# Both batches of a head side by side in the query and key rooms, fetched together for the first tile

## The reference, cut to what matters

```python
# L1 attention: 16 heads of 8, two softmaxes for each head
Q, K, V = proj(Wq), proj(Wk), proj(Wv)
Q1, Q2 = split(Q); K1, K2 = split(K)
A1 = where(causal, Q1 @ K1.T * scaling, -inf)
A2 = where(causal, Q2 @ K2.T * scaling, -inf)
attn = softmax(A1) - lam * softmax(A2)
O = attn @ V          # then an rms norm and Wo
```

## Time and profile before

| | us |
|---|---|
| median of 3 runs | 503.64 (502.91 to 507.45) |
| the profiled execution | 507.12 |
| its span, first to last instruction | 505.1 |
| PE busy | 461.2 (91%) |
| DVE busy | 418.5 (83%) |
| ACT busy | 264.7 (52%) |
| POOL busy | 266.7 (53%) |

### The profile page before, as it was taken

How to read it: one execution, slowest core, us unless ns; L and a number is a source line. 1 busy time by engine, 2 the same in 40 slices (tenths; PEclk the granted TensorE clock), 3 DMA queues, 4 the chain that set the end, 5 groups by cost and what they waited for, 6 DMA issues and landing times.

```text
span 505.1 us, 8612 instructions
## 1 busy us (share of the span) xinstructions
PE 461.2 (91%) x3072; PEld 218.8 (43%) x3072; DVE 418.5 (83%) x844; ACT 264.7 (52%) x416; POOL 266.7 (53%) x229
## 2 busy tenths in 40 slices
PE   3998986989999999998989999997989989999994
PEld 2755353534445444443334544453333434443341
DVE  2735579889888978899999899977999995997794
ACT  1355641456677526447675533455755662466550
POOL 6311531245473649438677316533754686455982
PEclk9999999899999999999999999998999997999998
DMA  7800267830478360132285183101692077113101
GB/s 276 321 15 1 74 157 149 131 65 1 125 163 135 80 141 0 38 69 62 62 192 127 49 138 71 50 21 45 173 147 57 8 122 132 43 42 89 43 0 42
DMA packets 49890, 46.15 MB, mean 91 GB/s; under 512 B 6361, under 2 KB 39481, under 8 KB 49209
## 3 DMA queue, kind: packets, MB, share of 16 engines
q1 hardware_dynamic: 49848, 45.61, 39.6%
HBM read 37.47 MB, written 7.60 MB: 89 GB/s over the span
## 4 chain that ended last, share of the span: by engine, by line
PE 63%; DVE 21%; DMA 4%; issue 3%; POOL 3%; SPq 3%; ACT 2%; POOLq 1%; DVEq 0%; ACTq 0%
PE bank L778 9%; PE bank L769 7%; PE scores L809 7%; PE bank L790 6%; PE bank L864 4%; DVE nmax L1314 4%; PE scores L704 3%; PE scores L695 3%; PE scores L719 3%; PE scores L698 3%; PE scores L803 3%; DMA ka<-parts_scratch 2%; PE scores L743 2%; PE bank L869 2%; DVE h L1290 2%
## 5 line engine op out<-in xcount | busy, mean ns | idle before, releaser
L1106 POOL TENSOR_TENSOR gb<-gb,wb 128x512 f32<-128x512 f32 x64 | 84.5, 1320 | 103.7 <-ACT gb L1005 73.7
L1020 ACT ACTIVATE pk<-scores 128x1024 f32<-128x1024 f32 x96 | 95.5, 1023 | 48.6 <-PE scores L809 48.6
L1099 POOL TENSOR_SCALAR_AFFINE_SELECT pk<-pk 128x512 f32<-128x512 f32 (+1 forms) x96 | 80.1, 845 | 49.7 <-ACT pk L1020 49.6
L1002 ACT ACTIVATE gt<-bank,bgh 128x512 f32<-128x512 f32 (+1 forms) x68 | 46.8, 688 | 75.0 <-PE bank L769 58.6
L1314 DVE TENSOR_REDUCE nmax<-scores 128x8 f32<-128x1024 f32 x64 | 76.6, 1219 | 9.5 <-PE scores L809 9.2
L778 PE MATMUL bank<-xnt,wu 128*128 128x512 f32 x128 | 71.1, 638 | 2.2 <-DVE h L1297 2.1
L769 PE MATMUL bank<-xnt,wg 128*128 128x512 f32 x128 | 70.9, 637 | 0.4 <-ACT gb L1005 0.4
L790 PE MATMUL bank<-h,wd 128*128 128x512 f32 x128 | 68.3, 624 | 0.4 <-DVE h L1297 0.4
L1297 DVE SCALAR_TENSOR_TENSOR h<-bank,bu,h 128x512 f32<-128x512 f32 x64 | 48.1, 751 | 11.9 <-PE bank L778 9.9
L1290 DVE SCALAR_TENSOR_TENSOR h<-gt,gb 128x512 f32<-128x512 f32 x64 | 53.3, 832 | 1.0 <-PE bank L790 0.8
L1314 DVE TENSOR_REDUCE nmaxf<-scores 128x8 f32<-128x1024 f32 x32 | 39.0, 1219 | 7.3 <-PE scores L809 6.8
(11 more groups left out here) (259 smaller groups left out, 700.0 us busy)
## 6 DMA issues: line engine op xcount, KB each, us to landing
wb<-wt_scratch SPq DMA_DIRECT2D x64, 256.0 KB, 4.2
parts_scratch<-parts SPq DMA_DIRECT2D x48, 128.0 KB, 2.4
qa<-parts_scratch SPq DMA_DIRECT2D x32, 96.0 KB
ka<-parts_scratch SPq DMA_DIRECT2D x32, 96.0 KB
qa<-parts_scratch SPq DMA_DIRECT2D x32, 64.0 KB
ka<-parts_scratch SPq DMA_DIRECT2D x32, 64.0 KB
ha<-in_wkq SPq DMA_DIRECT2D x1, 1024.0 KB, 4.9
wb<-in_wvo SPq DMA_DIRECT2D x1, 1024.0 KB, 7.6
```

Of the source, the lines that this page charges most:

```text
L1002: A(gt[0:rows, c % 2, :], bank[5][0:rows, :], ACT.Tanh, bias=bgh[0:rows, j:j + 1], scale=0.5).then_inc(s_gate_act, 1)
L1020: A(dst.rearrange("p (h m) q -> p m h q", m=2), pairs[pair_of(step)][:, :, :].rearrange("p m (h q) -> p m h q", q=cols), ACT.Exp, scale=SC ...
L1099: pool.affine_select(out=dst, in_=dst, compare_op=ALU.is_ge, fill=0.0, base=0, pattern=[[0, heads], [1, P]], channel_multiplier=-1).then_i ...
L1106: pw(gb[:, c % 2, :], gb[:, c % 2, :], wb[:, k % 2, j % 2, :], ALU.mult).then_inc(s_ga_done, 1)
```

## The change

The rooms `qa` and `ka` have the head ahead of the batch, so that both batches of a head lie side by side, 1,024 bytes in each partition. For the first tile, `fetch/0/0` moves both batches at once: 24 transfers as before, each with the same number of rows, of 1,024 bytes instead of 512. `fetch/0/1` then moves nothing, and the first tile's wait for batch 1 looks at the semaphore of batch 0. For the other tiles each batch is fetched by itself as before, in rows of 512 bytes that now land 1,024 bytes apart. All else follows the new order of the indices.

```diff
-        qa = sb("qa", [P, CB, HEADS, SEQ], BF16)
-        ka = sb("ka", [P, CB, HEADS, SEQ], BF16)
+        qa = sb("qa", [P, HEADS, CB, SEQ], BF16)
+        ka = sb("ka", [P, HEADS, CB, SEQ], BF16)
...
                         b = rest[0]
-                        for f in range(2):
+                        both = c == 0
+                        for f in range(2 if b == 0 or not both else 0):
...
-                                        src = t["parts_dram"][c, n, heads, m, first * DH:(first + width) * DH, b * SEQ:(b + 1) * SEQ]
-                                        sp.dma_start(dst[row:row + width * DH, b, heads, :],
-                                                     src.rearrange("h r t -> r h t")).then_inc(s_qk_in[b][f], 16)
+                                        src = t["parts_dram"][c, n, heads, m, first * DH:(first + width) * DH, :]
+                                        if both:
+                                            sp.dma_start(dst[row:row + width * DH, heads, :, :].rearrange("r h b q -> r h (b q)"),
+                                                         src.rearrange("h r t -> r h t")).then_inc(s_qk_in[0][f], 16)
+                                        else:
+                                            sp.dma_start(dst[row:row + width * DH, heads, b, :],
+                                                         src[:, :, b * SEQ:(b + 1) * SEQ].rearrange("h r t -> r h t")).then_inc(s_qk_in[b][f], 16)
...
-                            sp.dma_start(qa[row:row + 3, b, :, :],
+                            sp.dma_start(qa[row:row + 3, :, b, :],
...
-                                  last = mm(s[m][:, h, :], stat[half, b, h0 + h, row:row + P], move[half, b, h0 + h, tile0:tile0 + width],
+                                  last = mm(s[m][:, h, :], stat[half, h0 + h, b, row:row + P], move[half, h0 + h, b, tile0:tile0 + width],
...
-                        pe.wait_ge(s_qk_in[b][g // 2], c * QK_IN + QK_IN)
+                        pe.wait_ge(s_qk_in[b if c else 0][g // 2], (c if b else c + 1) * QK_IN if c else QK_IN)
```

More of the change, by code:

```diff
@@ L603, in _ @@
                     row = m * HALF + TERMS
-                    sp.dma_start(dst[row:row + 2, :, :, :].rearrange("r b h q -> r (b h) q"),
+                    sp.dma_start(dst[row:row + 2, :, :, :].rearrange("r h b q -> r (h b) q"),
                                  rows[:, :].unsqueeze(1).to_broadcast([2, CB * HEADS, SEQ])).then_inc(s_room_rows, 16)
@@ L1076, in _ @@
                         pool.wait_ge(s_xn0, TILES)
-                        pool.memset(ka[:, :, :, :].rearrange("p b h q -> p (b h q)").bitcast(F32), TWO_ONES).then_inc(s_rooms, 1)
+                        pool.memset(ka[:, :, :, :].rearrange("p h b q -> p (h b q)").bitcast(F32), TWO_ONES).then_inc(s_rooms, 1)
                         pool.memset(v1[:, :, :, :], 0.0).then_inc(s_rooms, 1)
```

## The result

| | us |
|---|---|
| before, median of 4 | 504.23 (502.91 to 507.45) |
| after, median of 4 | 514.6 (513.21 to 516.71) |
| ratio after to before | 1.020, 95% interval 1.0137 to 1.0262 |
| profiled execution after, its span | 513.78, 511.8 |

The change costs some 10 us (7 to 13 by the interval), where 3 were forecast and 511.5 was the upper end of the range.

A forecast was written before the change was run, and what follows sets the result against it. The prediction took DVE's gapless maxima to bound the first tile's stretch, with fetches hidden. Later maxima (+4.6 us) less the vanished wait (-1.6) gave +3.0 on the median 503.64: 506.6 us, range 501 to 511.5.

The forecast's parts named there:

- What bounds the stretch: First tile's maxima: DVE works without a gap from 77.66 to 89.2 us, and both halves of the fetch are hidden.
- what is late next: First tile: first maximum 1.5 us late, the seventh 4.6 us late in all, paid in full by everything after.
- Layout and later tiles at zero: Tiles 1 to 3: 512-byte rows landing 1,024 bytes apart, and matmul operands in the new layout, taken to cost zero.
- I take 160 GB/s, between 143 and 175: First tile's joint fetch: assumed transfer rate, landing the halves at 78.5 and 88.4 us.
- the 90 that the prediction had named as a sign against itself: First tile's fetch: transfers ending after 90 us would show the prediction wrong, in favour of bytes alone.
- The slow end: Joint fetch: lower bound on the rate, time going by bytes at 143 GB/s in the mean.
- The "fast" witness: Same kind of fetch in tile 2: 175 GB/s over four microseconds, taken as what the transfers can do at least.
- bytes alone set the time: Rival, joint fetch at 143 GB/s: halves at 79.7 and 90.7, +5.3 us, +7.3 with the low clock; chance 0.30.
- The gain of 1.6 us: Before the first `score`: PE's 1.62 us wait for `qa<-mrows` vanishes without batch 1's fetch ahead; bounds 1.5 to 1.6 us.
- `wb/0`: covered, as forecast: First tile's routing weights: reload later, POOL through at 95.2, DVE needing it at 95.95, covered by 0.8 us.
- The clock at zero: PE's lower clock around the first tile's maxima: 1 to 1.5 us gained or 2 lost possible, taken as zero.
- Under the maxima it costs nothing: First tile's maxima: PE's lower clock costs nothing there, as DVE sets the pace.

The follow-up runs named there:

- e1: Kernel before with the changed kernel's room layout, every fetch still by itself in rows of 512 bytes: 504.93 us, ratio 1.000 to before.
- e7: Changed kernel with each of the joint fetch's 24 transfers covering 16 partitions and all eight heads (first tile's scores wrong): 511.52 us, one run.
- e9: Changed kernel with the joint fetch cut into 48 transfers of 8 partitions and all eight heads (first tile's scores wrong): 519.17 us, one run.
- e2: Changed kernel with the joint fetch cut into 48 transfers of 512-byte rows, same order of bytes and joint wait: 517.35 us, ratio 1.029 to before.
- e15: Changed kernel with 48 transfers of 512-byte rows, in each half batch 0's 12 transfers and then batch 1's 12: 511.86 us, one run.
- e14: Kernel before with every fetch's transfers taking partitions of the two halves in turn: 504.08 us, ratio 0.998 to before.
- e5: Kernel before with the first tile's batch 1 transfers moved right behind batch 0's, each batch awaited by itself: 510.18 us, ratio 1.011 to before.
- e6: Kernel before with the second half of batch 1's first-tile fetch moved behind wb/2: 509.81 us, ratio 1.011 to before.

## Why the prediction was wrong

- **What bounds the stretch, and what is late next: right.** Two waits appeared where they were forecast, at the first maximum and at group 2's, nothing filled them, and the second half's landing set the end. Layout and later tiles at zero: right, within the 2 us that e1 can tell.
- **The term that failed is the rate.** The step "I take 160 GB/s, between 143 and 175" put the halves at 78.5 and 88.4, 10.8 and 20.7 us after the first issue. They came after 16.0 and 25.8, at 125 GB/s in the first ten microseconds and 144 later. The seventh maximum was 9.7 us late instead of 4.6, and these 5.1 us are most of the miss: 9.7 - 1.6 = 8.1 us, 8.8 at the first `score`, against +3.0. The transfers ran until about 93 us, past the 90 that the prediction had named as a sign against itself.
- **The slow end was no bound.** "The time goes by bytes", 143 GB/s, was read from transfers half as long that SP issued at 0.4 us each. I took a rate seen at one load as the least that twice the load could get. The transfers of 16 and 8 partitions don't reach it (136 and about 100 GB/s, e7 and e9), and back to back for the same partitions they do worse still (e2 against e15). Of the 5.1 us, 1.6 are the two batches moved side by side (25.8 against e15's 24.2); the other 3.5 stay in e15, which is not far from the slow end (90.7 - 67.69 = 23.0). The "fast" witness, 175 GB/s over four microseconds in tile 2, came with the same mixture of 24, 16 and 8 partitions; why a stretch so short ran at the rate that here only 24 and 48 partitions hold (178 and 176) isn't shown.
- **The rival "bytes alone set the time" had the direction** and 509 to 511 us; the measured 514.6 lies beyond it, near the 516 that stood beside it as the estimate from the ports of the Trainium skill, "SBUF — State Buffer", "Door 1: The DMA port swizzle" (second half at 97.5; it was 93.9). It was given no chance of its own, as the fetch before was some 3 us quicker than that rule. The doubled fetch was quicker than it too, by 3.6 us.
- **The gain of 1.6 us: uncertain.** The wait for `qa<-mrows` is gone. But e1 and e14 fetch batch 1 ahead of the rows as the kernel before does, and they show no such wait either: PE starts the first `score` 5.03 us after that issue in both, straight from its step before, as in the changed kernel. The row of e14, to be read beside the earlier trace rows:

```profile
102.09 0.39 PE L808 MATMUL scores<-qa,ka 53*128 53x256 bf16 x4
```

So the 1.62 us may belong to the one execution that was profiled, or the layout of e1 and the order of e14 may each have removed it; there is no second profile of the kernel before. Against e14 the changed kernel's first `score` is 10.1 us late (44.24 against 34.17 after the first issue), which is nearly the 10.4 between the medians.

- **`wb/0`: covered, as forecast**, by 0.7 us (POOL through at 100.77, DVE at 101.50). e5 shows what is there without that cover.
- **The clock at zero: nearly right.** It was low for 20 us instead of 7. From the seventh maximum to the first `score` the changed kernel takes 17.8 us, the one before 17.1 without its wait: 0.7 us lost. "Under the maxima it costs nothing" was wrong in general: in e1, e5 and e6 DVE waited 1.42 us for PE at the lower clock under the maxima.
- **Open**: 8.8 us are traced to the first tile; the ratio's 7 to 13 us contain them. The 1.6 us up to the medians' 10.4 may be the wait that only one profile has, which isn't shown. Open too is the mechanism by which repeated transfers for the same partitions slow down.

## What to carry to other kernels

A longer row makes a transfer over few partitions hardly quicker by the byte: twice the bytes over 8 to 24 partitions took about twice the time. Joining transfers joins their waits, so the first user pays for bytes that only the second needs; check who waits for the first half before making it larger, and what small transfer (here the routing weights) stands behind it in the queue. A rate read at one load is not a floor for a larger one. And a wait seen in one profile is a gain to count on only if a second profile has it too.

## What the runs showed of the hardware that was not expected

- The same 3.1 MB in 48 transfers of 512-byte rows took 28.0 us to PE's second start when the two batches of the same partitions followed each other and 24.2 us when 12 transfers lay between them (105 against 147 GB/s).
- The DMA busy share doesn't tell the rate: 1.13 at 136 GB/s over 16 partitions, 0.83 at 178 over 24.
- SP's issuing slowed down in the doubled fetch: six issues that took 2.6 us before took 6.0. A slow landing alone doesn't do it: in e7, whose second half came about as late (25.3 us), the last six took 2.8. What does isn't shown.
- With PE filled, the granted clock stayed at 1.00 through twenty microseconds in which it was else 0.5 for half of the time, and the kernel wasn't quicker.
- The clock fell at different times in executions with the same steps up to there: at about 86 us in the kernel before and at about 77 in e6, where the maxima came 1.5 us later for it.
